# A norm by chunks beside the last sums of a gated block, and the first two sums of the next block among its last gates

## The chip, the cores and the metric

One core of a Trainium2 chip runs the whole program. The metric is device time in microseconds (us), from start to end of one execution; before the change it is 3267.45 us, the median of 3 runs (3265.71 to 3273.17). Five engines work side by side and wait for each other by semaphores: TensorE (PE), VectorE (DVE), ScalarE (ACT), GpSimd (POOL) and SyncE (SP), which here issues the transfers.

## The reference, cut to what matters

Four graph blocks are added to x, one after the other. Each begins with a layer norm of x and a relu. Two of them matter here: the gated block (L0) and the convolutions (L1).

```python
h = jnp.maximum(_layernorm(x, axis=-1), 0.0)
x = x + _L0_gnn_ref(h, edge_index, L0_gnn_weight, ...)   # gated block
h = jnp.maximum(_layernorm(x, axis=-1), 0.0)
x = x + _L1_gnn_ref(edge_index, h, L1_gnn_W0, ...)       # convolutions
...
# gated block, 4 layers, x is [3125, 128]
for l in range(NUM_LAYERS):
    m = x @ weight[l]
    agg = jax.ops.segment_sum(m[src], dst, num_segments=n_nodes)
    x = _gru_cell(agg, x, w_ih, w_hh, b_ih, b_hh)
# convolutions: a sum over edges, two products, a second sum over edges
x = jax.ops.segment_sum(h[src], dst, num_segments=N) + b0
```

## The kernel before, in words

The 3125 nodes are 25 tiles of 128 rows. The edges are a matrix of counts, kept in SBUF (`A`), so a sum over edges is a matrix product: for one chunk of destination nodes, 25 tiles times 2 halves (a number is kept as a high and a low 16-bit half), that is 50 matmuls into one PSUM bank. There are 7 chunks, of 4, 4, 3, 4, 3, 4 and 3 tiles, so 512, 512, 384, 512, 384, 512 and 309 columns; they are called chunks 0 to 6 below. Sums of even chunks go to bank 0, of odd ones to bank 1.

The order on each engine is written out by hand, and each engine runs its own list strictly in order. `block_gru` is the gated block, with layers 0 to 3. In layers 1 to 3, `sum_chunk` (PE) and `among` (DVE) walk over the 25 tiles of the sum of chunk ci+1, and the table `AMONG` says what else is done ahead of which tile for the gates of chunk ci: "a" keeps the finished sum (DVE, L1128), "b" the gates' products with the state (PE, L952), "c" those with the sum (PE, L962), and on DVE the whole rest of the gate (`gate_c`: L1146 and L1149, which give the argument of the tanh, then L1151, L1154 and L1156, the new state). "S" is one step of other work, `Symmetric`: PE transposes blocks of another matrix (L854) into bank 6 or 7, and DVE adds them (L873). A step on PE waits for the DVE step two before it, whose bank it takes. ACT does the sigmoids (L1055, L1057) and the tanh (L1059).

`finish` turns a chunk's new state into rows: PE transposes it into bank 7 (L757), ACT and DVE keep the two halves for the next layer (L1069, L1170), and in the last layer DVE adds it to `x_nodes` (L1166). Steps that use bank 7 wait for that. In layer 0 most sums were made earlier, so its gates stand close together: per chunk PE runs `gate_b`, a few tiles of the next layer's sum, a step, `gate_c`, `finish` of the chunk before, and a second step, which takes bank 7.

After layer 3 comes a barrier of all engines. `block_gcn`, the convolutions, begins with `Norm` (L188 to L229): DVE and ACT make the norm of x by groups of 4 tiles, into `g_h16`. PE waits for each group in its first sum (`norm.pe_split`), then makes the other six (L1279), each followed by the product with the first weight (L1292) of the chunk before.

## Time and profile before

| | |
|---|---|
| median of 3 runs | 3267.45 us |
| profiled execution | 3268.28 us, its span 3265.8 us |
| PE busy | 2968.8 us, 91% |
| DVE busy | 2186.7 us, 67% |
| ACT busy | 897.4 us, 27% |

The span runs from the first to the last instruction. Busy shares are means over many stages. Where a row ends in brackets, they give the idle time of the engine just before the instruction and what ended it.

### The profile page before, as it was taken

Reading aid. Unit: us, or ns where it says so; the run is one execution under the profiler, and the core shown is the slowest. Engines: PE = TensorE matmul, PEld = TensorE weight load, DVE = VectorE, ACT = ScalarE, POOL = GpSimd, SP = SyncE. Lnnn points to the kernel's source line nnn. Section 1 sums busy time; section 2 is a strip of 40 time slices with the busy share of each in tenths; the row PEclk is TensorE's granted clock in tenths of the full one; section 3 lists DMA queues with packets and bytes.
Section 4 is the critical chain, followed back from the end, with each engine's and each line's share of the span. In section 5 each row is a group of like instructions: output and inputs, shape, how many; then the busy total and the mean of one; then the engine's idle time right before and its main releaser. Section 6 shows DMA issues by size and latency. Waiting matters only on the chain. (4 is left out here: it accounts for less than half of the span.)

```text
span 3265.8 us, 47549 instructions
## 1 busy us (share of the span) xinstructions
PE 2968.8 (91%) x18761; PEld 1780.3 (55%) x18761; DVE 2186.7 (67%) x4024; ACT 897.4 (27%) x1685; POOL 16.7 (1%) x23
## 2 busy tenths in 40 slices
PE   2888779999897999999979999989999998999997
PEld 2566445555343554545545665655656564656665
DVE  7999445555326777776657666686667586666676
ACT  3888422111111000000023222233222233222222
POOL 2000000000000000000000000000000000000000
PEclk8999989999998999999989999999999999999999
DMA  5455247676004655554330000020000002000001
GB/s 125 147 149 160 82 143 224 219 225 196 22 1 138 175 153 167 166 160 126 100 114 3 4 3 4 3 81 4 3 7 4 3 17 69 3 4 3 4 3 41
DMA packets 310958, 265.84 MB, mean 81 GB/s; under 512 B 32767, under 2 KB 289409, under 8 KB 308174
## 3 DMA queue, kind: packets, MB, share of 16 engines
q1 hardware_dynamic: 296558, 259.28, 25.9%
q10 hardware_dynamic: 13760, 2.61, 0.4%
q8 instruction: 153, 2.51, 0.3%
q0 software_dynamic: 416, 0.85, 0.1%
q14 instruction: 71, 0.58, 0.1%
HBM read 172.67 MB, written 90.05 MB: 80 GB/s over the span
## 5 line engine op out<-in xcount | busy, mean ns | idle before, releaser
L1708 PE MATMUL psum<-r_wd,r_h 128*128 128x512 fp8e4 (+1 forms) x2600 | 568.0, 375 | 13.7 <-ACT r_h L229 13.4
L2283 PE MATMUL psum<-m_agg,m_weights 128*128 128x512 f16 (+2 forms) x2016 | 422.0, 362 | 33.3 <-ACT m_agg L2190 33.3
L2244 PE MATMUL psum<-counts,m_h 128*128 128x512 fp8e4 (+2 forms) x2100 | 417.5, 355 | 12.6 <-DVE m_h L1987 12.6
L2302 PE MATMUL psum<-m_weights,x_nodes 128*128 128x256 f16 (+1 forms) x3600 | 413.0, 273 | 17.0 <-DVE m_wtmp L2097 15.4
L1708 PEld LDWEIGHTS psum<-r_wd,r_h 128*128 128x128 f16 x2600 | 241.5, 97 | 307.5 <-issue 15.5
L2302 PEld LDWEIGHTS psum<-m_weights,x_nodes 128*128 128x128 f16 (+1 forms) x3600 | 350.1, 98 | 74.7 <-DVE m_wtmp L2097 22.1
L2283 PEld LDWEIGHTS psum<-m_agg,m_weights 128*128 128x128 f16 x2016 | 196.8, 101 | 241.2 <-issue 49.3
L2244 PEld LDWEIGHTS psum<-counts,m_h 128*128 128x128 f16 x2100 | 206.3, 98 | 210.3 <-issue 21.3
L2202 ACT ACTIVATE m_hT<-m_hT,m_g 128x256 f32<-128x256 f32 x300 | 135.4, 500 | 599.1 <-DVE m_hT L2111 599.1
L2190 ACT ACTIVATE m_agg<-psum,x_nodes 128x512 f32<-128x512 f32 (+2 forms) x336 | 236.3, 716 | 143.7 <-PE psum L2283 113.7
L2111 DVE SCALAR_TENSOR_TENSOR m_hT<-psum,x_nodes,m_bias 128x512 f32<-128x512 f32 (+1 forms) x150 | 112.0, 750 | 169.8 <-PE psum L2319 169.7
L2097 DVE SCALAR_TENSOR_TENSOR m_wtmp<-psum,x_nodes,m_bias 128x256 f32<-128x256 f32 (+1 forms) x300 | 144.9, 483 | 120.0 <-PE psum L2302 116.6
L2088 DVE TENSOR_TENSOR x_nodes<-m_agg,x_nodes 128x512 f16<-128x512 f32 (+2 forms) x336 | 209.8, 624 | 11.5
L2319 PE MATMUL psum<-m_weights,m_agg 128*128 128x512 f16 x900 | 206.5, 379 | 0.0
L679 PE MATMUL psum<-oh_c,oh_s 128*128 128x150 f16 x1566 | 156.1, 237 | 48.4 <-ACT counts L714 31.0
L873 DVE TENSOR_TENSOR sym_blocks<-sym_blocks,psum 128x1024 uint16<-128x1024 uint16 (+1 forms) x169 | 110.5, 665 | 117.9 <-PE psum L854 117.3
L679 PEld LDWEIGHTS psum<-oh_c,oh_s 128*128 128x128 f16 x1566 | 111.9, 100 | 111.6 <-issue 67.6
L713 ACT ACTIVATE strip<-psum 128x600 uint16<-128x600 f32 x239 | 162.4, 680 | 34.3 <-PE psum L679 32.3
L975 PE MATMUL psum<-counts,g_h16b 128*128 128x512 fp8e4 (+2 forms) x700 | 159.3, 359 | 2.7 <-DVE g_h16b L1170 2.7
L1279 PE MATMUL psum<-counts,g_h 128*128 128x512 fp8e4 (+2 forms) x700 | 138.4, 357 | 15.9 <-ACT g_h L229 15.3
L2100 DVE SCALAR_TENSOR_TENSOR m_h<-m_wtmp,m_g,m_h 128x256 f32<-128x256 f32 (+1 forms) x300 | 145.3, 484 | 10.7
L2086 DVE CAST x_nodes<-m_agg 128x512 f16<-128x512 f32 (+2 forms) x336 | 131.2, 390 | 17.0 <-ACT m_agg L2190 7.1
(298 smaller groups left out, 3275.6 us busy)
## 6 DMA issues: line engine op xcount, KB each, us to landing
r_wd<-packed_sym SPq DMA_DIRECT2D x120, 640.0 KB, 4.1
packed_counts<-strip SPq DMA_DIRECT2D x21, 1800.0 KB, 7.8
sym_blocks<-packed_counts SPq DMA_DIRECT2D x88, 384.0 KB, 4.6
packed_sym<-sym_blocks SPq DMA_DIRECT2D x84, 384.0 KB, 3.3
w_stage<-in_L_gnn_strong_W SPq DMA_DIRECT2D x12, 1024.0 KB, 6.7
m_weights<-in_L_gnn_strong_W SPq DMA_DIRECT2D x21, 512.0 KB, 4.7
x_parked<-x_nodes SPq DMA_DIRECT2D x2, 1600.0 KB, 5.9
x_nodes<-x_parked SPq DMA_DIRECT2D x2, 1600.0 KB, 6.3
```

What stands on the lines that cost most here:

```text
L679: m = pe.matmul(psum[:, unit_at(u, w):unit_at(u, w) + UC], oh_s[q][:, k, :, v], oh_c[q][:, k, :, v], start=True, stop=True)
L713: act.activation(typed_home, typed, ACT.Copy, scale=0.5).then_inc(kept_a, 1)
L975: m = pe.matmul(bank[bk][:, 0:cw], h16[l % 2][:, part, i, :], A[:, i, c_:c_ + cw], start=(i == 0 and part == 0), stop=(i == NT - 1 and par ...
L1708: m = pe.matmul(bank[pair[b]][:, 0:2 * cw], h16[:, part, p0 + i, :], f_[:, 2 * b:2 * b + 2, :], start=(p0 + i == 0 and part == 0), stop=(p ...
L2088: vec.tensor_tensor(s_[:, BANK:BANK + cw], wide32, s_[:, 0:cw], ALU.subtract).then_inc(s_split, 1)
L2097: vec.scalar_tensor_tensor(tmp[k % 2][0:r_, :], bank[6 + k % 2][0:r_, 0:H], k_strong[0:r_], bcast[0:r_, ge * H:(ge + 1) * H], ALU.mult, AL ...
L2100: vec.scalar_tensor_tensor(h2[0:r_, i, :], tmp[k % 2][0:r_, :], gates[ci % 2][0:r_, k, ge:ge + 1], h2[0:r_, i, :], ALU.mult, ALU.add).then ...
L2190: act.activation(agg[:, hh % 2, 0:cw], bank[4 + hh % 2][:, 0:cw], ACT.Relu, bias=b1s[:, e * FB + f:e * FB + f + 1], scale=k_hidden).then_i ...
L2244: m = pe.matmul(bank[kb][:, 0:cw], h16[:, part, i, kb * P:(kb + 1) * P], A[:, i, c_:c_ + cw], start=(i == 0 and part == 0), stop=(i == NT ...
L2283: m = pe.matmul(bank[4 + hh % 2][:, 0:cw], w_[:, i, kb, f * P:(f + 1) * P], agg16[:, j, kb, 0:cw], start=(x_ == 0), stop=(x_ == len(todo) ...
L2302: m = pe.matmul(bank[b_][0:r_, 0:H], s_[:, pa[0] * BANK + k * P:pa[0] * BANK + k * P + r_], w_[:, pa[1], f, :], start=(f == 0 and pa == PA ...
L2319: m = pe.matmul(bank[2 + pr % 2][0:r_, :], agg16[:, pa[0], kb, k * P:k * P + r_], w_[:, pa[1], kb, :], start=(y_ == 0), stop=(y_ == len(to ...
```

## The change

`ChunkNorm` makes the norm of one chunk in seven calls: four on DVE (center, vary, scale, low half) and three on ACT (square, root, high half). For chunks 0 to 3 they stand in the lists of DVE and ACT during layer 3's sums of chunks 3 to 6 (`NORM_AT`); for chunks 4 to 6 in a new list, `last_gates`, around the gates of chunk 6. PE's `last_gates` puts tiles 0 to 21 of the convolutions' first two sums (`pe_next_sum`) among those gates and behind them; tiles 22 to 24 follow the barrier. The DVE part of `gate_c` is split in `gated` and `state`; in layers 1 to 3 a step stands between the two ("Sd"), in layer 0 `finish` of the chunk before and a step. PE's gates wait for each bank on its own.

```diff
--- before.py
+++ after.py
...
+
+        def wide(self, k, j):
+            n_ = self.tiles(k)[1]
+            return self.st[:, j, 0:n_, None].to_broadcast([P, n_, D])
+
+        def dve_center(self, k):
+            s, n_ = self.tiles(k)
+            m = self.st[:, 0, 0:n_]
+            vec.tensor_reduce(m, xn[:, s, :], axis=AX.X, op=ALU.add).then_inc(steps.handle, steps.up())
+            settle()
...
+        def act_all(self, k):
+            self.act_square(k)
+            self.act_root(k)
+            self.act_high(k)
+
+        def dve_low(self, k):
+            s, n_ = self.tiles(k)
+            vec.wait_ge(ln_high, self.split + k + 1)
+            vec.scalar_tensor_tensor(self.h16[:, 1, s, :], self.hn[:, 0:n_, :], FIXED, self.h16[:, 0, s, :], ALU.mult,
+                                     ALU.subtract).then_inc(ln_low, 1)
+            vec.wait_ge(ln_low, self.split + k + 1)
+
+        def pe_split(self, k):
...
+    def pe_next_sum(ci, tiles, norm_):
+
+        c_, cw = CH[ci]
+        for i in tiles:
+            if i == 0:
+                pe.wait_ge(g_summed_low, NL * NCH - (NCH - 1 - ci) % 2)
+            if i == tiles_of(CH[chunk_of(i)])[0][0]:
+                norm_.pe_split(chunk_of(i))
+            for part in range(2):
+                m = pe.matmul(bank[ci % 2][:, 0:cw], g_h16[:, part, i, :], A[:, i, c_:c_ + cw],
+                              start=(i == 0 and part == 0), stop=(i == NT - 1 and part == 1))
+        if tiles[-1] == NT - 1:
+            m.then_inc(c_summed, 1)
...
-        AMONG = {1: "S", 3: "a", 4: "S", 6: "S", 7: "b", 9: "S", 11: "c", 13: "S", 16: "S", 19: "S", 22: "S"}
+        AMONG = {1: "S", 3: "a", 4: "S", 6: "S", 7: "b", 9: "S", 11: "c", 13: "Sd", 16: "S", 19: "S", 22: "S"}
...
+            next_norm = ChunkNorm(c, g_h16)
+
+            def center(k):
+                vec.wait_ge(g_low, (NL - 1) * NCH + k + 1)
+                next_norm.dve_center(k)
+
+            NORM_AT = {1: center, 7: next_norm.dve_vary, 16: next_norm.dve_scale, 20: next_norm.dve_low}
+
+            def normed_beside(l, ci):
+
+                return ci - 3 if l == NL - 1 and ci >= 3 else None
...
-                    if n:
-                        pe.wait_ge(g_reset_kept, n)
-                        pe.wait_ge(g_update_kept, n)
-                        pe.wait_ge(g_gated_sum, n)
-                    for g, bk in enumerate((BR, BZ, BH)):
+                    for g, (bk, left) in enumerate(((BR, g_reset_kept), (BZ, g_update_kept), (BH, g_gated))):
+                        if n:
+                            pe.wait_ge(left, n)
                         for t, (wp, hp) in enumerate(PAIRS_OF):
...
                     for g, (bk, made_of) in enumerate(((BR, g_reset), (BZ, g_update), (BI, g_input))):
+                        if bk == BI and n:
+                            pe.wait_ge(g_gated_sum, n)
...
+                def last_gates():
+
+                    l = NL - 1
+                    t = [tiles_of(ch)[0][0] for ch in CH]
+                    gate_b(l, LC)
+                    finish(l, LC - 1)
+                    pe_next_sum(1 - LC % 2, range(0, 5), next_norm)
+                    gate_c(l, LC)
+                    pe_next_sum(1 - LC % 2, range(5, t[LC - 2]), next_norm)
+                    pe_next_sum(LC % 2, range(0, 8), next_norm)
+                    finish(l, LC)
+                    pe_next_sum(LC % 2, range(8, t[LC - 2]), next_norm)
+                    for ci in range(2):
+                        pe_next_sum(ci, range(t[LC - 2], t[LC]), next_norm)
...
+                        beside = normed_beside(l, ci + 1) if ci < LC else None
+                        if beside is not None:
+                            next_norm.act_square(beside)
+                            next_norm.act_root(beside)
+                        if (l, ci) == (NL - 1, LC):
+                            next_norm.act_all(LC - 2)
                         gate_c(l, ci)
+                        if beside is not None:
+                            next_norm.act_high(beside)
                         if 0 < ci < LC:
...
+                for k in (LC - 1, LC):
+                    next_norm.act_all(k)
...
                             if what == "c" and gates_of is not None:
-                                gate_c(l, gates_of)
+                                gated(l, gates_of)
+
+                            if what == "d" and gates_of is not None:
+                                state(l, gates_of)
+                        if i in NORM_AT and normed_beside(l, ci) is not None:
+                            NORM_AT[i](normed_beside(l, ci))
+
+                def last_gates():
+
+                    l = NL - 1
+                    gate_a(l, LC)
+                    center(LC - 2)
+                    finish(l, LC - 1)
+                    next_norm.dve_vary(LC - 2)
+                    next_norm.dve_scale(LC - 2)
+                    gated(l, LC)
+                    next_norm.dve_low(LC - 2)
+                    center(LC - 1)
+                    state(l, LC)
+                    next_norm.dve_vary(LC - 1)
+                    next_norm.dve_scale(LC - 1)
+                    finish(l, LC)
+                    next_norm.dve_low(LC - 1)
+                    center(LC)
+                    next_norm.dve_vary(LC)
+                    next_norm.dve_scale(LC)
+                    next_norm.dve_low(LC)
...
-                    gate_c(0, ci)
+                    gated(0, ci)
                     if ci == 0:
+                        state(0, ci)
                         gate_a(0, EARLY + 1)
-                    if ci:
+                    else:
                         finish(0, ci - 1)
                         sym.dve_step()
+                        state(0, ci)
...
-                sum_chunk(False, 0)
-                pe.wait_ge(c_in, C_IN)
+                for ci in range(2):
+                    pe_next_sum(ci, range(tiles_of(CH[NCH - 1])[0][0], NT), norm)
                 for ci in range(NCH):
-                    if ci + 1 < NCH:
-                        sum_chunk(False, ci + 1)
+                    if ci + 2 < NCH:
+                        sum_chunk(False, ci + 2)
+                    if ci == 0:
+                        pe.wait_ge(c_in, C_IN)
...
-                norm.act()
-                act.wait_ge(c_in, C_IN)
-                for ci in range(NCH):
+                def summed(ci):
...
+                summed(0)
+                summed(1)
+                act.wait_ge(c_in, C_IN)
...
+                    if ci + 2 < NCH:
+                        summed(ci + 2)
...
-                norm.dve()
-                vec.wait_ge(c_in, C_IN)
+                vec.wait_ge(deg_in, 32)
```

PE's list at the end of the gated block, before. The names: `g_h16b` is the source of the sums in layer 3, `g_ht` the state, `gate_w` the gates' weights.

```order
L975 MATMUL psum<-counts,g_h16b 128x309 x24
L757 MATMUL psum<-ident,g_ht 128x128 x3
L952 MATMUL psum<-g_hn,gate_w_62 128x309 x9
L962 MATMUL psum<-g_ag_52,gate_w_62 128x309 x9
L757 MATMUL psum<-ident,g_ht 128x128 x7
L1279 MATMUL psum<-counts,g_h_8 128x512 x100
```

The same place after:

```order
L1076 MATMUL psum<-counts,g_h16b 128x309 x24
L832 MATMUL psum<-ident,g_ht 128x128 x3
L1051 MATMUL psum<-g_hn,gate_w_62 128x309 x9
L832 MATMUL psum<-ident,g_ht 128x128 x4
L969 MATMUL psum<-counts,g_h_8 128x512 x10
L1063 MATMUL psum<-g_ag_52,gate_w_62 128x309 x9
L969 MATMUL psum<-counts,g_h_8 128x512 x36
L832 MATMUL psum<-ident,g_ht 128x128 x3
L969 MATMUL psum<-counts,g_h_8 128x512 x54
L1434 MATMUL psum<-counts,g_h_8 128x384 x50
```

Of the 100 matmuls from `g_h_8` that stood behind the last transposes, 10, 36 and 54 now stand in three pieces (the last one on both sides of the barrier), the first ahead of the last gates' products with the sum (L962, now L1063).

DVE's list in the sum of chunk 6, layer 1, before. `g_t` and `g_r` belong to the gates of chunk 5, `sym_blocks` to the steps.

```order
L1146 SCALAR_TENSOR_TENSOR g_t_59<-psum,g_sc,g_r_55 128x512
L1149 TENSOR_TENSOR g_t_59<-g_t_59,psum 128x512
L1151 TENSOR_TENSOR g_t_59<-g_ht,g_n_61 128x512
L1154 TENSOR_TENSOR g_t_59<-g_t_59,g_z_57 128x512
L1156 TENSOR_TENSOR g_ht<-g_t_59,g_n_61 128x512
L873 TENSOR_TENSOR sym_blocks_45<-sym_blocks_45,psum 128x2x512 x3
```

After:

```order
L1270 SCALAR_TENSOR_TENSOR g_t_59<-psum,g_sc,g_r_55 128x512
L1273 TENSOR_TENSOR g_t_59<-g_t_59,psum 128x512
L948 TENSOR_TENSOR sym_blocks_45<-sym_blocks_45,psum 128x2x512
L1280 TENSOR_TENSOR g_t_59<-g_ht,g_n_61 128x512
L1283 TENSOR_TENSOR g_t_59<-g_t_59,g_z_57 128x512
L1285 TENSOR_TENSOR g_ht<-g_t_59,g_n_61 128x512
L948 TENSOR_TENSOR sym_blocks_45<-sym_blocks_45,psum 128x2x512 x2
```

One step moved ahead of the three instructions that make the new state.

DVE's list in layer 0, the gates of chunk 1, before; `g_h16b` here is the row form of the chunk before, `g_hn` holds the state's halves.

```order
L1146 SCALAR_TENSOR_TENSOR g_t_59<-psum,g_sc,g_r_55 128x512
L1149 TENSOR_TENSOR g_t_59<-g_t_59,psum 128x512
L1151 TENSOR_TENSOR g_t_59<-g_ht,g_n_61 128x512
L1154 TENSOR_TENSOR g_t_59<-g_t_59,g_z_57 128x512
L1156 TENSOR_TENSOR g_ht<-g_t_59,g_n_61 128x512
L1170 SCALAR_TENSOR_TENSOR g_h16b<-psum,g_h16b 128x512
L1137 SCALAR_TENSOR_TENSOR g_hn<-g_ht,g_hn 128x512
L873 TENSOR_TENSOR sym_blocks_46<-sym_blocks_46,psum 128x2x512
```

After:

```order
L1270 SCALAR_TENSOR_TENSOR g_t_59<-psum,g_sc,g_r_55 128x512
L1273 TENSOR_TENSOR g_t_59<-g_t_59,psum 128x512
L1299 SCALAR_TENSOR_TENSOR g_h16b<-psum,g_h16b 128x512
L1262 SCALAR_TENSOR_TENSOR g_hn<-g_ht,g_hn 128x512
L948 TENSOR_TENSOR sym_blocks_46<-sym_blocks_46,psum 128x2x512
L1280 TENSOR_TENSOR g_t_59<-g_ht,g_n_61 128x512
L1283 TENSOR_TENSOR g_t_59<-g_t_59,g_z_57 128x512
L1285 TENSOR_TENSOR g_ht<-g_t_59,g_n_61 128x512
```

The row form of the chunk before, and the step behind it, moved ahead of the new state.

## Rows read from the trace of the kernel before

**Rows 1.** who PE waited for, 420 to 1010 us; us in total, times, longest

```profile
PE psum L1279 <- ACT g_h L229: 15.3, 4, 11.9
PE psum L757 <- DVE x_nodes L1166: 3.5, 1, 3.5
```

**Rows 2.** timeline of PE, 775 to 850 us: start, us, engine line, count [idle before]

```profile
809.93 0.49 PE L757 MATMUL psum<-ident,g_ht 128*128 128x128 f32 x3
810.26 1.35 PE L952 MATMUL psum<-g_hn,gate_w 128*128 128x309 f16 x9
811.58 1.34 PE L962 MATMUL psum<-g_ag,gate_w 128*128 128x309 f16 x9
...
816.85 0.52 PE L757 MATMUL psum<-ident,g_ht 128*128 128x128 f32 x3 [3.48 <-DVE x_nodes L1166]
829.23 3.21 PE L1279 MATMUL psum<-counts,g_h 128*128 128x512 fp8e4 x8 [11.87 <-ACT g_h L229]
...
839.63 10.59 PE L1279 MATMUL psum<-counts,g_h 128*128 128x512 fp8e4 x48 [1.03 <-ACT g_h L229]
```

**Rows 3.** timeline of PE, 855 to 926 us

```profile
856.10 1.02 PE L1292 MATMUL psum<-c_ag,c_w 128*128 128x512 f32 x2
...
904.38 1.02 PE L1292 MATMUL psum<-c_ag,c_w 128*128 128x512 f32 x2
906.50 0.79 PE L1292 MATMUL psum<-c_ag,c_w 128*128 128x309 f32 x2 [1.10 <-ACT c_ag L1317]
```

**Rows 4.** groups of instructions on DVE, 818 to 842 us (the norm)

```profile
L188 DVE TENSOR_REDUCE ln_st<-x_nodes 128x4 f32<-128x512 f32 (+1 forms) x7 | 4.4, 623 | 0.3 <-PEq L104 0.3
L198 DVE TENSOR_SCALAR ln_st<-ln_st 128x4 f32<-128x4 f32 (+1 forms) x7 | 1.2, 170 | 0.2
```

**Rows 5.** timeline of all engines, 819 to 826 us (ACT's part of the norm)

```profile
821.45 0.63 ACT L221 ACTIVATE ln_sq<-g_hn 128x512 f32<-128x512 f32 x1 [0.90 <-DVE g_hn L192]
822.10 1.28 ACT L225 ACT_TABLE_LOAD   x1
823.39 0.21 ACT L225 ACTIVATE ln_st<-ln_st 128x4 f32<-128x4 f32 x1
```

**Rows 6.** who PE waited for, 452 to 812 us

```profile
PE psum L854 <- DVE sym_blocks L873: 13.8, 13, 1.8
```

**Rows 7.** timeline of all engines, 771 to 780 us (sum of chunk 4, layer 3)

```profile
772.06 0.69 DVE L1149 TENSOR_TENSOR g_t<-g_t,psum 128x512 f32<-128x512 f32 x1
772.21 0.60 PE L854 MATMUL psum<-ident,sym_blocks 128*128 128x128 f32 x4
773.63 0.69 DVE L1151 TENSOR_TENSOR g_t<-g_ht,g_n 128x512 f32<-128x512 f32 x1 [0.88 <-ACT g_n L1059]
775.69 1.28 DVE L873 TENSOR_TENSOR sym_blocks<-sym_blocks,psum 128x1024 uint16<-128x1024 uint16 x2
776.52 0.63 PE L854 MATMUL psum<-ident,sym_blocks 128*128 128x128 f32 x4 [1.33 <-DVE sym_blocks L873]
```

**Rows 8.** busy time by stretch: us, PE, PEld, DVE, ACT, POOL, granted clock, DMA share, GB/s

```profile
370.00:447.00 77.00, 52.72 (x248) 28.93 (x247) 39.39 (x65) 23.34 (x40) 0.00 (x0) 0.84 0.25 81
690.00:797.00 107.00, 100.60 (x596) 61.28 (x595) 56.74 (x90) 16.21 (x26) 0.00 (x0) 1.00 0.70 223
812.00:830.00 18.00, 2.65 (x17) 1.55 (x15) 14.82 (x33) 7.43 (x13) 0.00 (x0) 0.67 0.28 96
```

**Rows 9.** who PE waited for, 370 to 450 us (layer 0)

```profile
PE psum L854 <- DVE g_h16b L1170: 24.3, 6, 4.5
```

**Rows 10.** timeline of all engines, 379 to 385 us (layer 0, gates of chunk 1)

```profile
381.96 0.57 ACT L1069 ACTIVATE g_h16b<-psum 128x512 f16<-128x512 f32 x1
383.63 0.68 DVE L1170 SCALAR_TENSOR_TENSOR g_h16b<-psum,g_h16b 128x512 f16<-128x512 f32 x1
384.46 0.78 PE L854 MATMUL psum<-ident,sym_blocks 128*128 128x128 f32 x4 [4.37 <-DVE g_h16b L1170]
```

**Rows 11.** DMA issues, 800 to 860 us: line, KB, us to landing

```profile
c_dinv<-dinv_row SPq DMA_DIRECT2D x1, 1562.5 KB, 7.6
```

More of the change, by code:

```diff
@@ L261, in act, with __init__, tiles, act_square @@
                 act.activation(self.ht[:, s.start * P:s.start * P + n_], bank[6 + g % 2][:, 0:n_], ACT.Copy).then_inc(rows_kept, 1)
+    class ChunkNorm:
+        def __init__(self, ctx, h16):
+            self.h16 = h16
+            self.hn, self.sq = (sbuf(ctx, n_, [P, LT, D], F32) for n_ in ("ln_hn", "ln_sq"))
+            self.st = sbuf(ctx, "ln_st", [P, 3, LT], F32)
+            self.base, self.split = ln_stages["n"], ln_stages["split"]
+            ln_stages["n"] += NCH
+            ln_stages["split"] += NCH
+        def tiles(self, k):
+            i0, n_ = chunk_rows(CH[k])[1:]
+            return slice(i0, i0 + n_), n_
+        def wide(self, k, j):
[6 more added lines that the diff above has]
+            settle()
+            vec.tensor_scalar(m, m, 1.0 / D, None, ALU.mult).then_inc(steps.handle, steps.up())
+            settle()
+            vec.tensor_tensor(self.hn[:, 0:n_, :], xn[:, s, :], self.wide(k, 0), ALU.subtract).then_inc(ln_centered, 1)
+        def act_square(self, k):
+            n_ = self.tiles(k)[1]
+            act.wait_ge(ln_centered, self.base + k + 1)
+            act.activation(self.sq[:, 0:n_, :], self.hn[:, 0:n_, :], ACT.Square).then_inc(ln_squared, 1)
+        def dve_vary(self, k):
+            n_ = self.tiles(k)[1]
+            v = self.st[:, 1, 0:n_]
+            vec.wait_ge(ln_squared, self.base + k + 1)
+            vec.tensor_reduce(v, self.sq[:, 0:n_, :], axis=AX.X, op=ALU.add).then_inc(steps.handle, steps.up())
+            settle()
+            vec.tensor_scalar(v, v, 1.0 / D, EPS, ALU.mult, ALU.add).then_inc(ln_varied, 1)
+        def act_root(self, k):
+            n_ = self.tiles(k)[1]
+            act.wait_ge(ln_varied, self.base + k + 1)
+            act.activation(self.st[:, 2, 0:n_], self.st[:, 1, 0:n_], ACT.Sqrt).then_inc(ln_rooted, 1)
+        def dve_scale(self, k):
+            n_ = self.tiles(k)[1]
+            hn, r = self.hn[:, 0:n_, :], self.st[:, 2, 0:n_]
+            vec.wait_ge(ln_rooted, self.base + k + 1)
+            vec.reciprocal(r, r).then_inc(steps.handle, steps.up())
+            settle()
+            vec.scalar_tensor_tensor(hn, hn, 0.0, self.wide(k, 2), ALU.max, ALU.mult).then_inc(ln_scaled, 1)
+        def act_high(self, k):
+            s, n_ = self.tiles(k)
+            act.wait_ge(ln_scaled, self.base + k + 1)
+            act.activation(self.h16[:, 0, s, :], self.hn[:, 0:n_, :], ACT.Copy, scale=FIXED).then_inc(ln_high, 1)
+        def act_all(self, k):
[3 more added lines that the diff above has]
+        def dve_low(self, k):
+            s, n_ = self.tiles(k)
+            vec.wait_ge(ln_high, self.split + k + 1)
[3 more added lines that the diff above has]
+        def pe_split(self, k):
+            pe.wait_ge(ln_high, self.split + k + 1)
+            pe.wait_ge(ln_low, self.split + k + 1)
@@ L1149, in gate_c, with state @@
                     vec.tensor_tensor(t_, t_, bank[BI][:, 0:cw], ALU.add).then_inc(g_gated_sum, 1)
+                def state(l, ci):
+                    n, q = l * NCH + ci, ci % 2
+                    c_, cw = CH[ci]
+                    h_, z_, t_, n_ = ht[:, c_:c_ + cw], zz[q][:, 0:cw], tt[q][:, 0:cw], nn[q][:, 0:cw]
                     vec.wait_ge(g_new, n + 1)
@@ L1206, in dve_gru @@
                             among(l, ci + 1, gates_of=ci)
-                        else:
-                            gate_a(l, ci)
-                            gate_c(l, ci)
+                        elif l < NL - 1:
+                            gate_a(l, ci)
+                            gated(l, ci)
+                            state(l, ci)
+                        else:
+                            last_gates()
                         if 0 < ci < LC:
@@ L1241, in block_gcn @@
             sc = sbuf(c, "c_sc", [P, 4], F32)
[L1242 removed]
             ag, tt, oo = ([sbuf(c, f"c_{n_}{i}", [P, BANK], F32) for i in range(2)] for n_ in ("ag", "t", "o"))
[L1244 removed]
+            C_IN = 64
             def sp_gcn():
@@ L1317, in act_gcn @@
                     act.activation(ag[q][:, 0:cw], bank[q][:, 0:cw], ACT.Copy, scale=1.0 / FIXED / COUNT_SCALE).then_inc(c_summed_kept, 1)
+                summed(0)
+                summed(1)
+                act.wait_ge(c_in, C_IN)
+                for ci in range(NCH):
+                    q, cw = ci % 2, CH[ci][1]
                     act.wait_ge(c_mixed, ci + 1)
```

31 lines of the change are left out of this document (11 added, 20 removed).

## The prediction, made before the changed kernel ran

> **What bounds the kernel now.** I read the engines' busy shares first: PE works 91% of the span, so an edit is worth what it takes out of PE's idle or slow time. I then asked who PE waited for, stretch by stretch. Three places belong to this change. (1) Behind the gated block PE waits for the norm: 15.3 us for ACT's high halves in four waits, the longest 11.9, and 3.5 for the last rows [rows 1]. The timeline shows it: the last gates' products end at 812.9 us, and the first two sums of the convolutions, 100 matmuls, end at 856.1 [rows 2, 3]. (2) In layers 1 to 3 PE waits 13.8 us in 13 places for a DVE step [rows 6]. (3) In layer 0 it waits 24.3 us in six places for DVE's row form [rows 9]. All three are waits for engines that aren't full (DVE is busy 56.74 of 107 us in layer 3 [rows 8]), so they come from the order of the lists.
>
> **Part 1, the end of the gated block.** I lay the new lists out on the old time axis, from the end of layer 3's last sum, 809.93 us [rows 2]. Durations for a full chunk: each of DVE's five wide norm instructions is .68, each of its three narrow ones .17 [rows 4]; ACT's square or high half .63, a change of table 1.28, the root .21 [rows 5]. DVE instructions of 384 and 309 columns I take at .56 and .48, in proportion, as estimates from these.
>
> DVE now carries, in the sum of chunk 6, the norm of chunk 3 (5 x .68 + 3 x .17 = 3.9 us) beside its own work. The center and vary parts fit in its waits; scale and low come behind the new state and end near 812.5, so the rows of chunk 4 are added near 813.0, not at 811. PE comes to the transposes of chunk 5 at 811.6 and needs the bank these rows leave: a new wait of about 1.5 us. Then PE runs 10 matmuls (a full-clock matmul is 10.59/48 = .22, less its tail .213 [rows 2]), the gates' products (1.34), 36 matmuls, and is at 824.7.
>
> Meanwhile the chain of DVE and ACT, in list order: center of chunk 4 to 814.8, rows of chunk 5 to 815.4, square, change of table and root to 816.9, scale to 817.7, high half to 818.3, table back to 819.6, then the sigmoid, DVE's two gated instructions and the tanh to 822; center of chunk 5 to 823.4, new state of chunk 6 to 824.9. So PE's last transposes start at 825.0, a wait of .3, and end at 825.5. The remaining 14 + 28 matmuls before the barrier take 9.0: 834.5. The norm of chunk 5 is complete at 828.3 (PE asks for it at 829.8), that of chunk 6 at 832.9, 1.6 before PE is through. Barrier .3, 12 matmuls 2.6: both sums are done at 837.4 instead of 856.1. Gain 18.7. Bounds: with no new wait at all, 835.7, gain 20.4; with three dearer table changes (below), about 16.
>
> The transfers of the convolutions move behind the new barrier, near 835. The largest, the inverse degrees, lands 7.6 us after issue [rows 11]: 843, and DVE first multiplies by it after the third sum and a product, near 848. Hidden by 5 us. It is no longer in the way of PE's products, which need only the small weights.
>
> One cost comes behind. The products with the first weight now follow two sums late, so behind the last sum stand three instead of two. Before, that tail ran from 904.38, with 1.10 idle, to a last product at 906.50 [rows 3]. Now the last product needs a keep on ACT that waits behind the bias of chunk 4, and DVE has three chunks to scale and reduce instead of one and a half. I count +.6, between 0 and 1.2 (one more chunk on DVE, two instructions of .56).
>
> **Part 2, the step ahead of the state.** [rows 7] show the mechanism: PE's step of 772.21 is ready for DVE at 772.8, but DVE waits for the tanh and makes the state, and adds the step at 775.69; PE's step two later waits 1.33 for it. Now the step stands ahead of the tanh's users. It is done near 773.6, in time that DVE waited anyway, so its wait goes. Next late is the step behind the state: in chunks of 512 and 384 columns it is done as PE comes for it, in that of 309 about .6 after. A layer has waits of .5, 1.3, 1.3 and 1.8 there (4.9): I keep 4.3 for layers 1 and 2 each, 8.6. In layer 3 the norm's scale and low parts stand between the last steps. In the sum of chunk 4 they put the last step, whose bank the transposes need, 1.5 us late, which eats the 1.3 won there. The other two waits go: 1.8. Sum 10.4; bounds 0 and 13.8.
>
> **Part 3, layer 0.** PE's second step waits for DVE's row form of the chunk before, at 383.63, but ACT's half for it is ready at 381.96 + .57 [rows 10]: DVE was making the state. With the new order DVE starts at 382.6, PE at 383.4. From ACT's ends and DVE's starts the six places give 1.05, .6, 1.2, .65, 1.2 and .35: 5.0 of the 24.3. The rest is the chain over sigmoid, tanh and ACT's two halves, which the change leaves alone. The state is made 3 us later, behind a step; its next user, PE's transposes, comes over 4 us after. The waits bank by bank I cost at nothing: no wait in front of L952 shows in [rows 1, 6], so none of the three was last.
>
> **Sum.** 18.7 - .6 + 10.4 + 5.0 = 33.5. The profiled execution took 3268.28 (span 3265.8 and 2.5 around it): 3234.8. It lies .8 above the median of the runs: 3234.0.
>
> **The rule against it.** ACT changes its table between root and sigmoid, ten times more than before, three of them in the chain above. In the trace the load takes 1.28 and the root starts .01 behind it, the square having ended .02 ahead [rows 5]: 1.3 for a change. The Trainium skill ("ScalarE: Activation LUTs", "What ACT_TABLE_LOAD costs") puts a drain of about 1380 ns on top, 2.66 us a change. By that rule the chain grows by 3 x 1.4 = 4.1, an estimate from that page, and the result would be some 3237; this case's trace shows no such drain.
>
> **Rivals.**
> A: the clock. From 370 to 447 us PE's granted clock is .84 on the mean, a mixture of its two levels, 1.2 and 2.4 GHz: after each 4 us wait the next products run slow [rows 8]. That is 77 x .16 x 2 = 25 us at the low level, of which half, 12, is lost. If the shorter waits of layer 0 leave the clock up, up to half of that comes back: 3228. For: the waits fall from 3.5-4.5 to 2.7-3.4. Against: they stay long.
> B: the chain at the block's end is slower than laid out (table changes, or semaphores between 14 handovers). It is DVE's and ACT's, PE has 1.6 to spare; beyond that each us counts: 3 to 5 us more, 3238.
> C: the norm makes DVE the bound in layer 3. It adds 3.9 + 3.9 + 3.2 + 3.9 = 15 to 57 in 107 us, 67% in all. If it stands in front of steps at the wrong moment each time, PE pays most of it: 15 + 1.8 lost, 3251.
> D: the end is not filled (the change doesn't do what it says): PE's list stands at the rows of chunk 5, and the norm chain is paid in full, about 8 us a chunk for chunks 4 to 6 (3.9 on DVE, 1.5 on ACT, 2.6 for tables): part 1 brings nothing, 3253.
> E, the other side: the lists lock into each other in layer 3. ACT's root is ahead of the sigmoid and waits for DVE's vary, which waits for square; DVE's scale is behind the state. If each pass through that loop is paid by PE in full, four chunks at 8 us and D's three make 56, against 33.5: 3290. It decides once a loop is longer than PE's lead of two banks plus the tiles between, some 5 us; DVE's idle time in these sums, 50 in 107, speaks against.
>
> **How the numbers follow.** Forecast .60, A .13, B .12, C .07, D .05, E .03. The predicted time is 3234. The range of 8 in 10 is 3225 to 3247: A below, B and half of C above, with the bounds of parts 1 and 2. Runs of this kernel differ by about .2%, 6.5 us, so less can't be told from none. All cases but E are faster by more: faster .96, same .02, slower .02.
>
> **What would show it.** Right: in the profile after, no wait over 2 us for ACT's high halves behind the block; 36 matmuls of the next sum in one run behind the last gates; the first convolution product some 30 us earlier than 856.1, allowing for the third sum now ahead of it (+8.3); PE's waits for DVE steps from 13.8 to about 4; layer 0's from 24.3 to about 19; ACT's table loads up by ten, each 1.28. Wrong: PE waits for steps over 10 us in layer 3, a wait over 3 us at the last transposes or at the barrier, or a second product with weights late because its transfer moved.

## The result, and the profile after

| | before | after |
|---|---|---|
| median (us) | 3267.19 (3265.71 to 3273.17, 4 runs) | 3229.03 (3227.63 to 3232.69, 4 runs) |
| profiled execution, span (us) | 3268.28, 3265.8 | 3232.69, 3230.8 |
| ratio of after to before | 1 | 0.9882, 95% interval 0.9867 to 0.9898 |

The change makes the kernel 38.2 us faster by the medians and 35.6 by the two profiled executions. The forecast was 3234.0, in a range of 3225 to 3247.

To find where the time went, I cut both timelines at the same instructions: the first matmul of the gates' products in each chunk (L952 before, L1051 after), then the third sum and the second sum of the convolutions.

| stretch (us) | before | after | difference | forecast |
|---|---|---|---|---|
| layer 0, first gates to layer 1's | 90.04 | 84.68 | -5.4 | -5.0 |
| layer 1 | 127.79 | 123.05 | -4.7 | -4.3 |
| layer 2 | 128.22 | 123.44 | -4.8 | -4.3 |
| layer 3, to the last chunk's gates | 97.45 | 95.14 | -2.3 | -1.8 |
| last gates to both first sums done | 45.84 | 27.12 | -18.7 | -18.7 |
| from there to the second sum | 56.98 | 56.66 | -0.3 | +0.6 |

They add up to 36.3. The first gates themselves come 1.7 later after (368.45 against 366.76), ahead of anything that the change touches. Another 0.4 is won behind these stretches, and 0.6 in what an execution takes beside its span; together that is the 35.6 of the two executions.

The end of the gated block first, where the change is largest. The timeline of PE after, from the last gates to the second sum (start, us, engine, line, count, idle before):

```profile
794.43 0.49 PE L832 MATMUL psum<-ident,g_ht 128*128 128x128 f32 x3
794.76 1.35 PE L1051 MATMUL psum<-g_hn,gate_w 128*128 128x309 f16 x9
797.68 0.63 PE L832 MATMUL psum<-ident,g_ht 128*128 128x128 f32 x4 [1.57 <-DVE x_nodes L1295]
798.15 2.32 PE L969 MATMUL psum<-counts,g_h 128*128 128x512 fp8e4 x10
800.31 1.35 PE L1063 MATMUL psum<-g_ag,gate_w 128*128 128x309 f16 x9
801.49 7.93 PE L969 MATMUL psum<-counts,g_h 128*128 128x512 fp8e4 x36
809.26 0.52 PE L832 MATMUL psum<-ident,g_ht 128*128 128x128 f32 x3
809.61 9.23 PE L969 MATMUL psum<-counts,g_h 128*128 128x512 fp8e4 x42
819.29 2.75 PE L969 MATMUL psum<-counts,g_h 128*128 128x512 fp8e4 x12 [0.45 <-PEq L104]
821.88 8.29 PE L1434 MATMUL psum<-counts,g_h 128*128 128x384 fp8e4 x50
830.00 1.02 PE L1449 MATMUL psum<-c_ag,c_w 128*128 128x512 f32 x2
...
869.51 2.59 PE L1449 MATMUL psum<-c_ag,c_w 128*128 128x384 f32 x6
875.92 1.97 PE L832 MATMUL psum<-ident,c_t 128*128 128x128 f32 x8 [3.83 <-DVE c_t L1517]
878.54 3.57 PE L1434 MATMUL psum<-counts,g_h 128*128 128x512 fp8e4 x8 [0.65 <-ACT g_h L1489]
```

L969 is the matmul in `pe_next_sum`. In [rows 2] PE stood still for 3.48 and 11.87 us here. Now 10, 36 and 42 matmuls of the next block run in the holes, and only 12 stand behind the barrier. The one new wait is 1.57 us for the rows of chunk 4, as laid out (1.5). DVE's last instruction of the norm shows how close the other side is:

```profile
815.75 0.56 DVE L315 SCALAR_TENSOR_TENSOR ln_hn<-ln_hn,ln_st 128x384 f32<-128x384 f32 x1
816.89 0.56 DVE L330 SCALAR_TENSOR_TENSOR g_h<-ln_hn,g_h 128x384 f16<-128x384 f32 x1 [0.59 <-ACT g_h L320]
```

It ends at 817.45 and PE's matmuls at 818.84, so DVE and ACT are 1.4 us ahead at the barrier (forecast 1.6).

Who PE waited for, 420 to 1010 us after (us in total, times, longest); this answers to [rows 1, 6]:

```profile
PE psum L929 <- DVE g_h16b L1299: 11.0, 4, 3.3
...
PE psum L832 <- DVE x_nodes L1295: 1.6, 1, 1.6
...
PE psum L832 <- issue: 1.3, 1, 1.3
PE psum L929 <- issue: 1.1, 2, 0.5
PE psum L929 <- DVE sym_blocks L948: 0.9, 2, 0.5
...
PE psum L1434 <- ACT g_h L1489: 0.7, 1, 0.7
```

The 15.3 us for ACT's high halves are gone, and the waits for DVE's step fell from 13.8 in 13 places to 0.9 in 2 (2.0 with the two at L929 that are listed as "issue", that is, with no releaser found). The 1.3 at L832 is the wait in the sum of chunk 4 of layer 3 that the forecast put at 1.5. The busy times answer to [rows 8], in the same order of columns; the granted clock is the third number from the end. First the 77 us of layer 0, after:

```profile
370.00:447.00 77.00, 56.88 (x267) 31.35 (x265) 39.53 (x66) 23.83 (x41) 0.00 (x0) 0.82 0.29 90
```

Its clock is about as it was (0.84). The other two stretches are cut here at the same instructions, layer 3 up to the last gates and the 18 us behind them, before:

```profile
712.81:810.26 97.45, 94.32 (x578) 59.22 (x577) 52.58 (x82) 15.81 (x24) 0.00 (x0) 1.00 0.66 213
810.26:828.26 18.00, 3.62 (x27) 2.39 (x24) 14.32 (x32) 7.11 (x13) 0.00 (x0) 0.72 0.29 100
```

and after:

```profile
699.62:794.76 95.14, 93.82 (x577) 59.49 (x576) 64.77 (x112) 30.97 (x42) 0.00 (x0) 1.00 0.69 220
794.76:812.76 18.00, 16.43 (x88) 8.41 (x86) 13.01 (x29) 9.27 (x14) 0.00 (x0) 1.00 0.00 0
```

In layer 3 DVE carries 12.2 us more, and PE is busy for a larger share, not a smaller one. Behind the last gates PE is busy 16.43 of 18 us instead of 3.62, at a granted clock of 1.00 instead of 0.72.

Layer 0, answering to [rows 9]: 24.3 us of waits in six places are now

```profile
PE psum L929 <- DVE g_h16b L1299: 19.4, 6, 3.4
```

### The profile page after: what moved, and what is told of

It is laid out like the page before. It is cut to its first block and busy times, and to the rows that moved or that the text cites. A ratio compares the mean times of both kernels' runs of the same rounds, so it can differ in the third digit from the quotient of the medians.

```text
span 3230.8 us, 47504 instructions
## 1 busy us (share of the span) xinstructions
PE 2968.3 (92%) x18761; PEld 1785.9 (55%) x18761; DVE 2186.6 (68%) x4024; ACT 909.9 (28%) x1695; POOL 16.8 (1%) x23
## 5 line engine op out<-in xcount | busy, mean ns | idle before, releaser
L2465 PE MATMUL psum<-m_weights,x_nodes 128*128 128x256 f16 (+1 forms) x3600 | 413.0, 273 | 17.0 <-DVE m_wtmp L2260 15.3
L1871 PEld LDWEIGHTS psum<-r_wd,r_h 128*128 128x128 f16 x2600 | 240.6, 96 | 307.8 <-issue 15.5
L2251 DVE TENSOR_TENSOR x_nodes<-m_agg,x_nodes 128x512 f16<-128x512 f32 (+2 forms) x336 | 209.8, 624 | 11.6
L1966 DVE SCALAR_TENSOR_TENSOR x_nodes<-psum,r_dg,x_nodes 128x128 f32<-128x128 f32 (+1 forms) x200 | 70.1, 350 | 106.0 <-PE psum L1823 100.6
```

The lines of the kernel that those rows point to most:

```text
L1871: m = pe.matmul(bank[pair[b]][:, 0:2 * cw], h16[:, part, p0 + i, :], f_[:, 2 * b:2 * b + 2, :], start=(p0 + i == 0 and part == 0), stop=(p ...
L2251: vec.tensor_tensor(s_[:, BANK:BANK + cw], wide32, s_[:, 0:cw], ALU.subtract).then_inc(s_split, 1)
L2465: m = pe.matmul(bank[b_][0:r_, 0:H], s_[:, pa[0] * BANK + k * P:pa[0] * BANK + k * P + r_], w_[:, pa[1], f, :], start=(f == 0 and pa == PA ...
```

## The experiments

Ten kernels were run, each with runs of the kernel before beside it. Their medians of the kernel before lie between 3268.07 and 3268.56. The intervals of the ratios are about 0.3% wide, that is 5 us to either side, so two experiments less than some 5 us apart are told apart by their traces alone, if at all.

**Without part 1.** The kernel before with parts 2 and 3 and the waits by bank.

```diff
 # before.py, with from after.py: gated()/state() apart, "Sd" at tile 13,
 # layer 0's new order, the three waits by bank
-                                gate_c(l, gates_of)
+                                gated(l, gates_of)
+                            if what == "d" and gates_of is not None:
+                                state(l, gates_of)
```

> The kernel before with only parts 2 and 3: the step ahead of the state, layer 0's order, the waits bank by bank. The norm and all seven sums of the convolutions stand behind the barrier as before. Theory: part 1 is worth 19 us by itself and the others about 17, so some 3250 (3267.2 - 17), and PE waits about 12 us again for ACT's first high half. It also shows what the norm costs in layer 3: without it the sum of chunk 4 should have no wait at its end, so layer 3 gains about 3.1 + .4 instead of the 2.3 that the trace after shows. Rival: the parts depend on each other (the filled end hides delays that the new order only moves there), then this kernel is above 3256 or below 3244.

Measured: 3246.72 (3244.61 to 3247.06), ratio 0.9932 (0.9915 to 0.9948). Part 1 brings 17.7 of the 38.2 us, and the rival's bounds (above 3256, below 3244) aren't reached. PE waits 14.3 us for ACT's high halves again, the longest 11.9, and both sums are done 45.8 us behind the last gates. Layer 3 is 93.67 long against 95.14: the norm beside the sums costs PE 1.5 us there.

**Part 1 without the filling.** The norm stays among the last gates, but TensorE's matmuls of the next sums all go behind the barrier.

```diff
                     finish(l, LC - 1)
-                    pe_next_sum(1 - LC % 2, range(0, 5), next_norm)
                     gate_c(l, LC)
-                    pe_next_sum(1 - LC % 2, range(5, t[LC - 2]), next_norm)
-                    pe_next_sum(LC % 2, range(0, 8), next_norm)
                     finish(l, LC)
-                    pe_next_sum(LC % 2, range(8, t[LC - 2]), next_norm)
-                    for ci in range(2):
-                        pe_next_sum(ci, range(t[LC - 2], t[LC]), next_norm)
...
-                    pe_next_sum(ci, range(tiles_of(CH[NCH - 1])[0][0], NT), norm)
+                    pe_next_sum(ci, range(NT), norm)
```

> The changed kernel with the norm where it stands, but no matmul of the first two sums of the convolutions among the last gates: all of both sums run behind the barrier. Which of the two halves of part 1 brings its 18.7 us? Theory (the filling): VectorE's last operation of the norm ends 22.7 us behind the last gates' first matmul, as in the changed kernel; the barrier follows, and then TensorE has all 100 matmuls of 0.21 us to do that now stand ahead of it, 21 us. The third sum begins some 44 to 46 us behind the last gates (27.1 in the changed kernel, 45.8 in the kernel before), and the time is 3229.0 + 18 to 19 = 3247 to 3248: the early norm alone brings nothing, since the old one already ran piece by piece ahead of the first sum. Rival (the early norm brings a good part by itself, since with the norm done TensorE needs no wait of 3.2 us between the blocks of its first sum, and VectorE has no matmuls' halves to wait for): the norm ends 5 us or more sooner, the third sum begins 36 to 40 us behind the last gates, and the time is 3238 to 3242.

Measured: 3248.94 (3247.85 to 3256.28), ratio 0.9941 (0.9928 to 0.9955). The timeline of PE of this kernel:

```profile
797.85 1.35 PE L1051 MATMUL psum<-g_hn,gate_w 128*128 128x309 f16 x9
...
812.31 0.90 PE L832 MATMUL psum<-ident,g_ht 128*128 128x128 f32 x3 [9.72 <-DVE g_ht L1279]
821.08 23.10 PE L969 MATMUL psum<-counts,g_h 128*128 128x512 fp8e4 x100 [7.86 <-PEq L104]
844.01 6.18 PE L1428 MATMUL psum<-counts,g_h 128*128 128x384 fp8e4 x37
```

Both sums are done 46.2 us behind the last gates, 45.8 before the change. The early norm alone brings nothing: PE stands still for 9.72 us during the chain and for 7.86 at the barrier, and then does all 100 matmuls, 88 of which the filling puts into the gaps. All of part 1's gain is the filling. It needs the early norm, since those matmuls read its output.

**The step behind the state again (part 2 undone).**

```diff
-11: "c", 13: "Sd"
+11: "cd", 13: "S"
```

> The changed kernel with the new state made directly behind the gated part in layers 1 to 3, ahead of the step, as before the change. Theory: the 4.7 us that each of layers 1 and 2 gained come back, and with the norm beside them layer 3 loses more than its 2.3, since vary and scale now stand behind a late state as well: 3229 + 12 to 15, that is 3241 to 3244, and PE's waits for DVE steps are near 14 us or above. Rival: the step's place is worth only layer 1 and 2's listed waits (8.7): 3238.

Measured: 3245.78 (3243.44 to 3247.60), ratio 0.9929 (0.9912 to 0.9945): part 2 is worth 16.7 by the medians, which is above the 12 to 15 expected. The traces say 4.7, 4.9 and 2.9 for layers 1, 2 and 3 and 0.3 at the end, 12.9 together, and who PE waited for, 440 to 800 us, has the old row back, word for word in its numbers:

```profile
PE psum L929 <- DVE sym_blocks L948: 13.8, 13, 1.8
```

The 3.8 us between the two is less than medians can tell.

**Layer 0's order undone (part 3).**

```diff
                     gated(0, ci)
+                    state(0, ci)
                     if ci == 0:
-                        state(0, ci)
                         gate_a(0, EARLY + 1)
-                    else:
+                    if ci:
                         finish(0, ci - 1)
                         sym.dve_step()
-                        state(0, ci)
```

> The changed kernel with layer 0's old order on DVE (gated, state, rows of the chunk before, step). Theory: 5.1 us come back, 3234, and the six waits for the row form rise from 19.4 to 24.3; the granted clock in layer 0 stays about as low. Rival A of the prediction (the clock): if the shorter waits had kept the clock up, more than 5 would come back, 3237 or above.

Measured: 3236.38 (3234.78 to 3238.64), ratio 0.9905 (0.9888 to 0.9921), 7.4 more than with part 3, between the theory's 5.1 and the rival's 8. The waits are back at 24.3 us. In its trace layer 0 is 87.47 long, 2.8 more than after. It is not the 90.04 of before, because the layer's same 306 matmuls took less time in this execution: PE is busy 61.95 us in it, 64.06 in that of after and 64.52 in that of before. So 4.9 us more of waits stand against 2.1 less of slow matmuls.

**The waits by bank undone.**

```diff
+                    if n:
+                        pe.wait_ge(g_reset_kept, n)
+                        pe.wait_ge(g_update_kept, n)
+                        pe.wait_ge(g_gated_sum, n)
...
-                        if bk == BI and n:
-                            pe.wait_ge(g_gated_sum, n)
```

> The changed kernel with the gates' waits for the three banks at once, ahead of gate_b, as before the change. Theory: none of them is ever the last wait, so nothing changes: 3229, within .2%. Rival: in the end of the block, where the last gates' products with the state follow the last sum directly, or in layer 0, the wait for the gated sum would be last: 3230 to 3233, with a wait in front of L1051 in the profile.

Measured: 3229.96 (3226.58 to 3233.32), ratio 0.9886 (0.9870 to 0.9902): worth nothing, as forecast. The waits in layer 0 are the same 19.4, 6, 3.4, yet in its trace the layer is 77.50 long, 7.2 less than after. Busy time from 370 to 447 us (the clock is the third number from the end; [rows 8] have 0.84 for before), first of the kernel with layer 0's old order, then of this one:

```profile
370.00:447.00 77.00, 52.73 (x255) 28.95 (x254) 39.39 (x65) 23.36 (x40) 0.00 (x0) 0.87 0.28 87
```

```profile
370.00:447.00 77.00, 56.40 (x304) 32.48 (x303) 42.87 (x71) 24.43 (x42) 0.00 (x0) 0.93 0.32 100
```

With one and the same set of waits (19.3 or 19.4 us, the longest 3.4) layer 0 took from 77.5 us (clock 0.93) to 84.7 (0.82) in the profiled executions of seven kernels. One execution doesn't tell what layer 0 costs.

**ACT's high halves early in layer 0.** What is left of the waits there ends with ACT's copy of the rows, which stood behind the tanh. Here ACT makes the state's high half ahead of the sigmoids and the rows' between the second sigmoid and the tanh.

```diff
-                def gate_c(l, ci):
+                def gate_c(l, ci, between=None):
...
+                    if between is not None:
+                        between()
                     act.wait_ge(g_gated_sum, n + 1)
...
-                    gate_c(0, ci)
+                    if ci:
+                        act.wait_ge(g_state, ci)
+                        state_high(ci - 1, g_state_high)
+                    gate_c(0, ci, between=(lambda: row_high(0, ci - 1)) if ci else None)
                     if ci == 0:
                         gate_a(0, EARLY + 1)
-                    if ci:
-                        finish(0, ci - 1)
```

> The changed kernel with ACT's order in layer 0 changed: the high half of the state ahead of the sigmoids, the high half of the rows between the second sigmoid and the tanh, where ACT is idle. DVE's row form can then start right behind the gated sum, some 1.6 to 2 us earlier per chunk. Theory: the six waits fall from 19.4 to about 9 us, so 10 us less by the waits alone (3219), and since the waits are then near 1.5 us, the granted clock of layer 0 stays up and up to 12 us more come back: 3210 to 3219. It tells whether it is the length of the waits that makes the slow products behind them (in one run of an earlier kernel with the same 19.4 us of waits layer 0 took 77.5 us at a mean clock of .93, in the others 84 to 85 at .82). Rival: the slow products come with every wait: then exactly the waits' 10 us, and the clock stays near .82.

Measured: 3211.21 (3210.16 to 3215.21), ratio 0.9827 (0.9814 to 0.9841), 17.8 us below the changed kernel. The waits of layer 0 are

```profile
PE psum L929 <- DVE g_h16b L1307: 9.1, 6, 1.6
```

and the layer is 63.29 long, 21.4 less than after, with layers 1 to 3 unchanged. Only 10.3 of the 21.4 are waits. The rest is the clock. Busy time in the whole of layer 0, of after and of this kernel:

```profile
368.45:453.12 84.67, 64.06 (x306) 35.44 (x306) 43.00 (x72) 25.23 (x43) 0.00 (x0) 0.84 0.29 91
```

```profile
367.18:430.47 63.29, 52.48 (x306) 30.98 (x306) 42.75 (x72) 26.18 (x43) 0.00 (x0) 1.00 0.39 122
```

PE is busy 11.6 us less with the same 306 matmuls, at a clock of 1.00 instead of 0.84, while DVE takes the same time and ACT 1 us more. The 10.3 and 11.6, less one new wait of 0.5 ahead of a transpose, are the 21.4. The two timelines of PE at the same work show it, first of after:

```profile
397.23 0.44 PE L929 MATMUL psum<-ident,sym_blocks 128*128 128x128 f32 x2 [3.22 <-DVE g_h16b L1299]
397.47 3.79 PE L1051 MATMUL psum<-g_hn,gate_w 128*128 128x512 f16 x9
```

and of this kernel:

```profile
389.81 0.41 PE L929 MATMUL psum<-ident,sym_blocks 128*128 128x128 f32 x2 [1.57 <-DVE g_h16b L1307]
390.06 2.11 PE L1051 MATMUL psum<-g_hn,gate_w 128*128 128x512 f16 x9
```

The same nine products take 3.79 us behind a wait of 3.22 and 2.11 behind one of 1.57.

**The tiles of the filling split.** On top of that kernel: of the three or four tiles that fill a chunk of layer 0, all but the first two stand behind the turn to nodes.

```diff
-                    for i, _ in tiles_of(CH[ci - 2]) if ci >= 2 else ():
+                    behind = [i for i, _ in tiles_of(CH[ci - 2])] if ci >= 2 else []
+                    for i in behind[:2]:
                         sum_tile(1, 0, i)
                     sym.pe_step(other)
                     gate_c(0, ci)
                     finish(0, ci - 1)
+                    for i in behind[2:]:
+                        sum_tile(1, 0, i)
                     sym.pe_step(other)
```

> On top of the kernel with ScalarE's two high halves moved early in layer 0: there TensorE still waits for VectorE's low halves six times, 9.1 us in all (1.6 us each), ahead of the second symbolic step. Here two of the three or four tiles of the next layer's first sum that fill TensorE's time in each chunk stand behind the turn to nodes and so ahead of that wait (4 matmuls, 0.9 us), and no longer all ahead of the first step. Theory (the wait is TensorE running out of work): five of the six waits shrink by 0.9 us, no new wait comes ahead of the first step, and the time falls by 4 to 5 us, to 3206 to 3207. Rival (in layer 0 the chain through VectorE and ScalarE now sets the length of a chunk, whatever TensorE does between): the waits turn up ahead of the first step or of the gates, layer 0 stays at 63.3 us, and the time stays within 1 us of 3211.

Measured: 3210.47 (3206.73 to 3213.22), ratio 0.9821 (0.9808 to 0.9835). The waits fall to

```profile
PE psum L929 <- DVE g_h16b L1310: 5.8, 6, 1.6
```

and layer 0 to 60.03, 3.3 less. So in the trace the wait is PE running out of work, and the rival is wrong for the layer. The 4.5 us expected counted two tiles in each of five chunks; the code moves eight tiles in all, 16 matmuls of 0.21 us, which are 3.4. The medians differ by 0.7, which can't be told from none, so no gain in device time is shown. The two profiled executions differ by 2.1: 3.3 are won in layer 0, but the first gates start at 369.02 and in that of the kernel above at 367.18. They lie between 365.9 and 372.9 in all profiles, with nothing of the change ahead of them. Where that comes from wasn't studied.

**The next sum first among the last gates.** Ten matmuls ahead of the transposes that wait 1.57 us.

```diff
-                    finish(l, LC - 1)
                     pe_next_sum(1 - LC % 2, range(0, 5), next_norm)
+                    finish(l, LC - 1)
```

> The changed kernel with PE's first 10 matmuls of the next sum ahead of the transposes of chunk 5 instead of behind them. Theory: PE's 1.57 us wait for the bank goes, since the 10 matmuls (2.1 us) cover it; the barrier waits for PE (818.8), DVE being through at 817.4, so nearly all of it is kept: -1.4, 3227.6, in the trace the third sum starts 25.6 instead of 27.1 us after the last gates' first product. Rival: the rows of chunk 5 come .6 later, the chain of DVE and ACT behind them sets the end, and nothing changes.

Measured: 3227.53 (3225.11 to 3233.06), ratio 0.9873 (0.9858 to 0.9888). The wait is gone at the first transposes and stands at the last, in the timeline of PE:

```profile
798.45 0.60 PE L832 MATMUL psum<-ident,g_ht 128*128 128x128 f32 x4
...
809.56 0.55 PE L832 MATMUL psum<-ident,g_ht 128*128 128x128 f32 x3 [1.56 <-DVE g_ht L1285]
```

The third sum begins 27.11 us behind the last gates, 27.12 after, as the rival said. The new state comes when DVE and ACT are through, wherever PE waits.

**The norm's scale and low parts at the end of each sum.**

```diff
-7: next_norm.dve_vary, 16: next_norm.dve_scale, 20: next_norm.dve_low
+7: next_norm.dve_vary, 22: next_norm.dve_scale, 23: next_norm.dve_low
```

> The changed kernel with the norm's scale and low parts behind the last step of a sum in layer 3 instead of between the last steps. Theory: the 1.3 us wait at the end of the sum of chunk 4 is made by them; it goes, layer 3 takes 93.8 instead of 95.14 us: 3227.7. Rival: DVE is then late for the next chunk (the rows, the first step and the centre stand behind the norm), and PE waits there instead: 3229 or more.

Measured: 3228.42 (3224.97 to 3233.62), ratio 0.9879 (0.9864 to 0.9894). Layer 3 is 94.92 long against 95.14: of the 1.5 that the norm costs, 0.2 comes back, where the theory had 1.3. PE's wait of 1.3 ahead of the transposes goes, and three of up to 0.3 for the node rows take its place, as the rival said.

**Three edits together.** ACT's early halves, the next sum first, and scale and low last.

```diff
 # the diffs of the early halves, of the next sum first and of scale and low last
...
+                    gate_c(0, ci, between=(lambda: row_high(0, ci - 1)) if ci else None)
...
+                    pe_next_sum(1 - LC % 2, range(0, 5), next_norm)
...
+22: next_norm.dve_scale, 23: next_norm.dve_low
```

> The three edits of this call together. Theory: they touch different stretches, so they add: 10 to 22 from layer 0, 1.4 and 1.3: 3204 to 3216. Rival: the end of the block is bound by DVE once layer 3 hands over with DVE late, and only layer 0's part is seen.

Measured: 3214.88 (3212.72 to 3217.30), ratio 0.9834 (0.9821 to 0.9848). Layer 0 is 63.30 and layer 3 94.91, so the two small edits add nothing that can be seen: the third sum begins 27.3 us behind the last gates. The median is 3.7 above that of the kernel with the early halves alone, less than medians can tell. The two profiled executions differ by 5.5, and the first gates are later by about as much (372.93 against 367.18).

## Why the prediction was right, and where a step was not

- **The sum.** Forecast 33.5, measured 36.3 in the stretches: 2.8 more, of which 1.4 in the layers, 0.9 in the tail and 0.4 in layer 0. The median after is 5.0 below the forecast of 3234.0; the other 2.2 lie between the two profiled executions and the medians.
- **The end of the block.** Forecast 18.7, measured 18.7, by the chain that was laid out from [rows 2, 4, 5]: DVE and ACT bring the new state and the last norm, PE fills. It came out step by step. With 15.5 added, the way from 794.76 to 810.26, the last transposes start at 824.8 (forecast 825.0), DVE's norm ends at 833.0 (832.9), PE's matmuls at 834.3 (834.5), and both sums are done at 837.4 (837.4). The durations of .56 and .48 for narrower chunks were called proportional, which would give .51 and .41; the values themselves are what the trace after has. The largest transfer, issued at 820.0, came in time: DVE first multiplies by the inverse degrees at 831.9 and had waited for ACT there. The run without filling shows that the gain is PE's work moved into 9.7 and 7.9 us of waiting; the run with the next sum first shows that the chain, not PE's order, sets the end. Rival D (the end not filled) has its price confirmed: not filling costs 19.9 by the medians (3248.94 against 3229.03), where it said 19 (3253 against 3234).
- **The tail.** The step "behind the last sum stand three instead of two ... I count +.6" failed: measured -0.3. The stretch behind the last sum did grow, from 8.70 to 9.03, and DVE's longer part is as counted: PE waits 3.83 for it instead of 3.17. But the 1.10 idle ahead of the last product [rows 3] is gone, which pays for the third product. And I added that product behind and did not take it away in front: between the sums stand four groups of products where [rows 3] end five, and from the first sums' end to the last sum's end it is 47.63 instead of 48.28.
- **The step ahead of the state.** The waits came as forecast: 13.8 us became 2.0, with the new one of 1.3 in the sum of chunk 4, so 10.5 net for a forecast of 10.4. The layers gave 4.7, 4.8 and 2.3, that is 11.8. What I had not counted is in PE's busy time, from the first gates of layer 1 to the last gates, before and then after:

```profile
456.80:810.26 353.46, 331.70 (x2012) 206.00 (x2011) 191.39 (x306) 65.89 (x108) 0.00 (x0) 1.00 0.69 218
```

```profile
453.12:794.76 341.64, 330.17 (x2011) 206.91 (x2010) 203.36 (x336) 81.05 (x126) 0.00 (x0) 1.00 0.72 226
```

The same matmuls (one record is missing) are busy 1.5 us less. In the trace the end of a matmul overlaps the start of the next by 0.16 us: the 36 matmuls after the last gates last from 801.49 to 809.42, and the next one starts at 809.26. A wait takes this overlap away, and there are 19 waits over 0.2 us before and 11 after, which makes 1.3 of the 1.5. In layer 3 the order alone is worth 3.8 (97.45 before, 93.67 without part 1), and the norm takes 1.5 of it back.
- **Layer 0.** The waits fell by 4.9, the 5.0 of the forecast. What part 3 is worth in time depends on the clock of the execution: 5.4 between the profiles of before and after, where PE is busy 0.5 less, 2.8 between after and the run without it, where PE is busy 2.1 more, 7.4 by their medians. The clock can move the layer by more than the part's size, and that the stretch came so near the forecast is in part luck.
- **Rival A, the clock.** In the profile after it did not come back (0.82 against 0.84), as the forecast said. But its mechanism is real. It put 12 us on the slow matmuls of layer 0 and let half of that come back. With waits of at most 1.6 us the clock is 1.00 and all of it comes back, 11.6 us, beside 10.3 of waits. The clock may also be why the medians fell by 38.2 where the stretches give 36.3: of the four executions after, the profiled one is the longest and has the lowest clock over the whole span (3232.69 us at 0.971; the others 3227.63 to 3229.87 at 0.973 to 0.975). Where in the span it differs was not recorded for those, so that stays argued.
- **Rivals B, C and E.** DVE is 1.4 us ahead at the barrier (B), PE pays 1.5 us for 15 of norm in layer 3 (C), and no wait passes 1.6 us there (E).
- **The tables.** ACT loads a table ten times more. The timeline of ACT after:

```profile
799.22 0.52 ACT L294 ACTIVATE ln_sq<-ln_hn 128x384 f32<-128x384 f32 x1 [2.67 <-DVE ln_hn L289]
799.76 1.28 ACT L307 ACT_TABLE_LOAD   x1
801.05 0.20 ACT L307 ACTIVATE ln_st<-ln_st 128x3 f32<-128x3 f32 x1
802.09 0.52 ACT L320 ACTIVATE g_h<-ln_hn 128x384 f16<-128x384 f32 x1 [0.84 <-DVE ln_hn L315]
802.63 1.28 ACT L1170 ACT_TABLE_LOAD   x1
803.93 0.61 ACT L1170 ACTIVATE g_r<-psum,g_b,g_sc 128x309 f32<-128x309 f32 x1
```

Each starts 0.02 behind the instruction before and ends 0.01 or 0.02 ahead of the next, 1.3 us a change. A drain of 1380 ns on top, by the Trainium skill ("ScalarE: Activation LUTs", "What ACT_TABLE_LOAD costs"), would make the chain some 4 us longer and the end of the block some 3, as an estimate. These rows, in which the next activation starts at once, and the measured 18.7 speak against it.

The kernel with the early halves beats both before and after: 3211.21, 1.7% below the kernel before. The one with the tiles split has the shortest layer 0 and the same time within what can be measured.

## What to carry to other kernels

A chain of small steps on two engines at a stage's end is worth hiding only if the third engine has work that needs none of it: moving the chain forward brought nothing here until 88 matmuls stood in its gaps. Look for where the operand of a waited-for instruction becomes ready and what its engine does in between: two reorderings of a list, the step ahead of the state and the copy ahead of the tanh, brought 13 and 18 us here. When a term of the sum moves between two places, write it down in both.

## What the runs showed of the hardware

- In layer 0, recurring waits of 3.1 to 3.4 us, 19.3 or 19.4 in all, go with a granted clock between 0.82 and 0.93 (370 to 447 us), that is a mixture of 1.2 and 2.4 GHz, from one execution to the next of programs that are the same there. The layer takes 77.5 to 84.7 us. With waits of at most 1.6 us (9.1 or 5.8 in all) the three profiled executions show 1.00 and 63.3, 63.3 and 60.0 us.
- So a wait can cost more than itself: 10.3 us less waiting made the layer 21.4 us shorter. No run has waits between 1.6 and 3.1 us there, and none tells whether the length of one wait or their sum counts.
- PE stood still for 9.72 us in the run without filling, and its next three transposes took 0.90 us instead of 0.52, at a granted clock of 0.50 (810 to 816 us), the lower of its two levels.
- A change of ACT's table took 1.28 us in each of the loads shown, and the next activation started 0.01 or 0.02 behind it where its operand was ready.
